# One row per routed token that carries weights and token number, two expert rows to a partition, loads ahead of the experts, and a sums buffer for each pair of batches

## The reference

```
probs = jax.nn.softmax(logits.astype(jnp.float32), axis=-1)
w_topk, sel = jax.lax.top_k(probs, K)
...
buf = jnp.zeros((E, CAP + 1, Hq), x.dtype).at[sorted_e, dest].set(x[tok])
g = jnp.einsum('ech,ehf->ecf', buf, w_gate)
u = jnp.einsum('ech,ehf->ecf', buf, w_up)
y = jnp.einsum('ecf,efh->ech', jax.nn.silu(g) * u, w_down)
wv = w_topk.reshape(-1)[order] * valid.astype(x.dtype)
out = jnp.zeros((T, Hq), x.dtype).at[tok].add(gath * wv[:, None])
sh = jax.nn.silu(x @ sw_gate) * (x @ sw_up) @ sw_down
sh = jax.nn.sigmoid(x @ w_shared_gate) * sh
```

## Time and profile before

| | us |
|---|---|
| median of 3 runs | 845.46 (843.39 to 845.92) |
| the profiled execution | 841.77 |
| its span in the profile | 839.5 |
| TensorE busy in it | 759.9 (91%) |
| VectorE, ScalarE, GpSimd busy | 544.3, 455.9, 493.8 |
| mean granted TensorE clock | 0.982 of full speed |

### The profile page before, as it was taken

How to read it: one execution, slowest core, us unless ns; L and a number is a source line. 1 busy time by engine, 2 the same in 40 slices (tenths; PEclk the granted TensorE clock), 3 DMA queues, 4 the chain that set the end, 5 groups by cost and what they waited for, 6 DMA issues and landing times.

```text
span 839.5 us, 12442 instructions
## 1 busy us (share of the span) xinstructions
PE 759.9 (91%) x3882; PEld 617.7 (74%) x3882; DVE 544.3 (65%) x1673; ACT 455.9 (54%) x1148; POOL 493.8 (59%) x400
## 2 busy tenths in 40 slices
PE   4688999999999999899999999999899858889957
PEld 2467888887888888788888788887676545667635
DVE  3398776688787978878787878895741223342433
ACT  4567876767876666697567777764521111111000
POOL 0445445453465588679578778857767555653560
PEclk9989999999999999999999999999999989999979
DMA  8906600000005010001301020403851299996270
GB/s 313 350 2 187 237 1 1 1 1 2 1 0 176 16 41 28 20 2 36 117 27 44 23 56 15 151 8 104 201 167 51 46 288 261 261 229 139 74 245 31
DMA packets 75152, 82.96 MB, mean 99 GB/s; under 512 B 8104, under 2 KB 65845, under 8 KB 75088
## 3 DMA queue, kind: packets, MB, share of 16 engines
q1 hardware_dynamic: 64208, 73.03, 28.3%
q0 software_dynamic: 9728, 8.46, 5.3%
q10 hardware_dynamic: 1152, 0.69, 0.3%
HBM read 54.37 MB, written 31.98 MB: 103 GB/s over the span
## 4 chain that ended last, share of the span: by engine, by line
PE 61%; DVE 14%; ACT 7%; issue 6%; DMA 6%; SPq 3%; POOL 2%; POOLq 0%; DVEq 0%; ACTq 0%
PE PJ L1271 17%; PE OUT L1369 9%; PE U L1358 5%; PE U L1324 5%; PE U L1515 4%; PE U L1347 4%; PE U L1359 2%; PE U L1323 2%; PE U L1271 2%; ACT U L521 2%; DMA xin<-in_dram 2%; DVE prob L927 2%; PE OUT L1460 2%; DMA xe<-slot_rows 2%; DVE U L917 2%
## 5 line engine op out<-in xcount | busy, mean ns | idle before, releaser
L709 POOL TENSOR_TENSOR qsw<-qsw,sinT 128x512 f32<-128x512 f32 x96 | 125.3, 1306 | 175.4 <-ACT qsw L508 174.2
L521 ACT ACTIVATE U<-U,nmax 128x128 f32<-128x128 f32 (+1 forms) x256 | 99.0, 387 | 94.5 <-DVE nmax L917 94.4
L1369 PE MATMUL OUT<-wo,oT 128*128 128x256 f32 x512 | 131.5, 380 | 0.0
L917 DVE CUSTOM_DVE_ANT_0 U<-U,mask 128x128 f32<-128x128 f32 (+1 forms) x256 | 86.6, 378 | 59.7 <-PE U L1324 59.3
L1271 PE MATMUL PJ<-hT_hi,w_hi 128*128 128x512 f32 x256 | 112.0, 437 | 0.8 <-issue 0.8
L1271 PE MATMUL PJ<-hT_lo,w_hi 128*128 128x512 f32 x256 | 101.3, 396 | 0.0
L1271 PE MATMUL PJ<-hT_hi,w_lo 128*128 128x512 f32 x256 | 101.0, 394 | 0.0
L713 POOL TENSOR_TENSOR qr<-qr,qsw 128x512 f32<-128x512 f32 x64 | 82.3, 1285 | 28.1 <-DVE qr L905 24.8
L927 DVE TENSOR_SCALAR prob<-U,rinv 128x128 f32<-128x128 f32 (+1 forms) x256 | 95.1, 413 | 4.5
L1369 PEld LDWEIGHTS OUT<-wo,oT 128*128 128x128 f32 x512 | 87.6, 191 | 6.6
L1358 PE MATMUL U<-pT,vN 128*128 128x256 f32 x256 | 78.3, 388 | 11.8 <-ACT pT L529 11.2
(11 more groups left out here) (199 smaller groups left out, 1651.8 us busy)
## 6 DMA issues: line engine op xcount, KB each, us to landing
wgu<-in_dram SPq DMA_DIRECT2D x32, 352.0 KB
expert_sum<-eq SPq DMA_DIRECT2D x3, 2176.0 KB, 17.8
sums<-expert_sum SPq DMA_DIRECT2D x12, 512.0 KB, 6.7
wd<-in_dram SPq DMA_DIRECT2D x16, 352.0 KB
wraw<-in_dram SPq DMA_DIRECT2D x8, 512.0 KB, 13.4
slot_rows<-eq SPq DMA_DIRECT2D x1, 4096.0 KB, 16.3
bcm<-mod_rows SPq DMA_DIRECT2D x8, 512.0 KB, 7.0
xe<-slot_rows SPq DMA_DIRECT2D x16, 256.0 KB, 8.3
```

Of the source, the lines that this page charges most:

```text
L521: last = act.activation(U[n % 3][:, a:z], U[n % 3][:, a:z], ACT.Exp, scale=-1.0, bias=nmax[:, n % 4, j:j + 1], accum_out=rsum[:, n % 4, j: ...
L709: pool.tensor_tensor(pair3(qsw[:, n % NQSW, :]), pair3(qsw[:, n % NQSW, :]), both(sinT[:, :]), ALU.mult).then_inc(t2_done, 1)
L917: last = dve.tensor_tensor_reduce(out=U[n % 3][:, a:z], in0=U[n % 3][:, a:z], in1=mask[:, a:z], scale=-float(HD) ** -0.5, scalar=3.4e38, o ...
L1369: last = pe.matmul(OUT[b][:, t * H:(t + 1) * H], oT[:, n % NOT, t * PN:(t + 1) * PN], wo[:, head, :], start=(head == 0 and t == 0), stop=( ...
```

## The change

The row that GpSimd scatters grows from 256 to 289 columns (ROW): the token's features, its 32 probabilities, its number as a float. The second scatter with all it needs (meta, eq, empty, post_pick, post_weights) goes. VectorE takes weight and number of two experts from the rows that were loaded (slot_w, slot_token, a semaphore told). An expert's weight rows 2p and 2p+1 now lie in partition p, which makes both next to each other in DRAM too; the transposes read every second column to match. SP's refill is split: rows, gate/up weights and down weights each wait for their own last use. gball and all four residual loads stand ahead of the wait for the scatters. sums and fin have a buffer for each pair; late_sums lies where the weight rings were. Beside it the zero fill writes rows of 1156 bytes.

```diff
+ROW = H + E + 1
+TOKEN = H + E
...
-            sp.dma_start(slots_d.rearrange("(a p) h -> p a h", p=PN),
-                         eq[:, 0:2, :, :].rearrange("p t k e -> p (t k e)").unsqueeze(1).broadcast_to([PN, E, H])).then_inc(st_zero, 16)
+            sp.wait_ge(fills, 9)
+            sp.dma_start(slots_d.rearrange("(s e) h -> s e h", e=E), blank[:, :].unsqueeze(1).broadcast_to([PN, E, ROW])).then_inc(st_zero, 16)
...
-            def expert_weights(e, i):
-
+            def gate_up_weights(e, i):
                 two = slice(2 * i, 2 * i + 2)
-                for dst, src in ((wgu[:, two, :, 0:F], w_gate), (wgu[:, two, :, F:2 * F], w_up)):
-                    sp.dma_start(dst.rearrange("p e c f -> p (e c) f"),
-                                 src[bass.ds(e, 2), :, :].rearrange("a (c p) f -> p (a c) f", p=PN)).then_inc(ld_e[i], 16)
-                sp.dma_start(wd[:, two, :, :].rearrange("p e c h -> p (e c) h"),
-                             w_down[bass.ds(e, 2), :, :].rearrange("a (c p) h -> p (a c) h", p=FH)).then_inc(ld_e[i], 16)
+                for g, src in enumerate((w_gate, w_up)):
+                    sp.dma_start(wgu[:, two, g, :, :].rearrange("p e c f -> p e (c f)"),
+                                 src[bass.ds(e, 2), :, :].rearrange("a (p c) f -> p a (c f)", p=PN)).then_inc(ld_gu[i], 16)
+
+            def down_weights(e, i):
+                two = slice(2 * i, 2 * i + 2)
+                sp.dma_start(wd[:, two, :, :].rearrange("p e c h -> p e (c h)"),
+                             w_down[bass.ds(e, 2), :, :].rearrange("a (p c) h -> p a (c h)", p=FH)).then_inc(ld_wd[i], 16)
...
             sp.wait_ge(st_base, 16 * NPAIR)
+            sp.wait_ge(st_xnt, 32 * NPAIR)
+            sp.wait_ge(lg_ps, NPAIR)
+            sp.dma_start(gball[:, :, :], mod_d[:, 3 * H:4 * H].partition_broadcast(PN)).then_inc(ld_gb, 16)
+            for q in range(NPAIR):
+                residual(q)
             sp.wait_ge(st_scat, 16 * NPAIR * TT * TOPK)
             for i in range(HALF):
                 slot_rows(2 * i, i)
-            sp.wait_ge(st_meta, 16 * NPAIR * TT * TOPK)
-            sp.dma_start(smeta[:, :, :].rearrange("p e c -> p (e c)"), meta_d.rearrange("(s e) c -> s (e c)", e=E)).then_inc(ld_meta, 16)
-            sp.dma_start(gball[:, :, :], mod_d[:, 3 * H:4 * H].partition_broadcast(PN)).then_inc(ld_gb, 16)
-            residual(0)
-            residual(1)
...
             for e in range(RING, E, 2):
+                i = (e // 2) % HALF
+                sp.wait_ge(xe_ps, e + 2 - RING)
+                sp.wait_ge(told, (e - RING) // 2 + 1)
+                slot_rows(e, i)
+                sp.wait_ge(gu_ps, e + 2 - RING)
+                gate_up_weights(e, i)
                 sp.wait_ge(ye_ps, e + 2 - RING)
-                slot_rows(e, (e // 2) % HALF)
-                expert_weights(e, (e // 2) % HALF)
+                down_weights(e, i)
...
-            expert_sums(0)
-            expert_sums(1)
             for q in range(NPAIR):
+                for i in range(NSUM):
+                    sp.dma_start(sums(q, i), acc_d[i][q * TOK:(q + 1) * TOK, :].rearrange("(t p) h -> p t h", p=PN)).then_inc(ld_sums[q], 16)
...
-            for c in range(TT * TOPK):
-                scatter_meta(LAST, c)
...
-                own(dve.tensor_tensor(ex[:, :, :], ex[:, :, :], red[:, 3, :].unsqueeze(2).broadcast_to([PN, TT, E]), ALU.mult))
+                dve.tensor_tensor(xn[:, :, H:H + E], ex[:, :, :], red[:, 3, :].unsqueeze(2).broadcast_to([PN, TT, E]), ALU.mult).then_inc(probs_done, 1)
...
+                    if n % 2 == 0:
+
+                        i = n % RING
+                        flat = xe[:, :, :].rearrange("p i r -> p (i r)")
+                        at = i * ROW + H + n
+                        dve.wait_ge(ld_xe[i // 2], 16 * (n // RING + 1))
+                        dve.tensor_copy(slot_w[:, n:n + 2], flat[:, at:at + ROW + 2:ROW + 1])
+                        dve.tensor_copy(slot_token[:, n:n + 2], xe[:, i:i + 2, TOKEN]).then_inc(told, 1)
...
-                        last = pe.transpose(PJ[n % 2][:, c * PN:(c + 1) * PN], xe[:, n % RING, c * PN:(c + 1) * PN], ident[:, :])
+                        last = pe.transpose(PJ[n % 2][:, c * PN:(c + 1) * PN], xe[:, n % RING, c:H:HC], ident[:, :])
```

More of the change, by code:

```diff
@@ L184, in adaln_block, with sums @@
         ye = sb("ye", [PN, RING, H])
-        smeta = sb("smeta", [PN, E, 2])
+        slot_w = sb("slot_w", [PN, E])
+        slot_token = sb("slot_token", [PN, E], I32)
         gball = sb("gball", [PN, B, H])
-        sums = sb("sums", [PN, 2, NSUM, TT, H])
-        fin = sb("fin", [PN, 2, TT, H])
+        fin = sb("fin", [PN, NPAIR, TT, H])
+        first_sums = sb("first_sums", [PN, NSUM, TT, H])
+        def sums(q, i):
+            return first_sums[:, i, :, :] if q == 0 else late_sums[:, q - 1, i, :, :]
         def bank(name):
@@ L443, in _ @@
                     sp.wait_ge(fin_done[q], 1)
-                    sp.dma_start(out[q * TOK:(q + 1) * TOK, :].rearrange("(t p) h -> p t h", p=PN), fin[:, q % 2, :, :]).then_inc(st_out[q % 2], 16)
+                    sp.dma_start(out[q * TOK:(q + 1) * TOK, :].rearrange("(t p) h -> p t h", p=PN), fin[:, q, :, :]).then_inc(st_out[q % 2], 16)
                 else:
@@ L447, in _ @@
                         sp.wait_ge(fin_done[q], t + 1)
-                        sp.dma_start(rows(out, q * TOK + t * PN), fin[:, q % 2, t, :]).then_inc(st_out[q % 2], 16)
[L449 to L452, removed]
+                        sp.dma_start(rows(out, q * TOK + t * PN), fin[:, q, t, :]).then_inc(st_out[q % 2], 16)
             sp.wait_ge(st_out[0], 16 * 2)
@@ L784, in _ @@
                 if l >= UNITS:
-                    for store, c in SCATTERS[l]:
-                        store(LAST - 1, c)
+                    for c in SCATTERS[l]:
+                        scatter(LAST - 1, c)
             post_base(LAST, 0)
@@ L828, in combine @@
             def combine(q):
-                a = sums[:, q % 2, 0, :, :]
-                pool.wait_ge(ld_sums[q % 2], 16 * NSUM * (q // 2 + 1))
+                a = sums(q, 0)
+                pool.wait_ge(ld_sums[q], 16 * NSUM)
                 for i in range(1, NSUM):
-                    own(pool.tensor_tensor(a, a, sums[:, q % 2, i, :, :], ALU.add))
+                    own(pool.tensor_tensor(a, a, sums(q, i), ALU.add))
                 own(pool.tensor_tensor(batches(a), batches(a), gate_of(q), ALU.mult))
-                f = fin[:, q % 2, :, :]
+                f = fin[:, q, :, :]
                 if q == 1:
@@ L1211, in expert_slot @@
                     dve.wait_ge(ye_ps, e + 1)
-                    if e == 0:
-                        dve.wait_ge(ld_meta, 16)
+                    dve.wait_ge(told, e // 2 + 1)
                     if e >= RING:
                         dve.wait_ge(st_acc[(e - RING) % NSUM], 16 * ((e - RING) // NSUM + 1))
-                    dve.tensor_scalar(ye[:, e % RING, :], YE[e % 2][:, 0:H], smeta[:, e, 0:1], None, ALU.mult).then_inc(ye_done, 1)
+                    dve.tensor_scalar(ye[:, e % RING, :], YE[e % 2][:, 0:H], slot_w[:, e:e + 1], None, ALU.mult).then_inc(ye_done, 1)
             def combine(q, step):
-                a = sums[:, q % 2, 0, :, :]
+                a = sums(q, 0)
                 if step < NSUM - 1:
                     if step == 0:
-                        dve.wait_ge(ld_sums[q % 2], 16 * NSUM * (q // 2 + 1))
-                    own(dve.tensor_tensor(a, a, sums[:, q % 2, step + 1, :, :], ALU.add))
+                        dve.wait_ge(ld_sums[q], 16 * NSUM)
+                    own(dve.tensor_tensor(a, a, sums(q, step + 1), ALU.add))
                 elif step == NSUM - 1:
@@ L1514, in expert_slot @@
                     for c in range(HC):
-                        last = pe.matmul(SC[e % 2][:, 0:2 * F], xeT[:, e % 2, c * PN:(c + 1) * PN], wgu[:, i, c, :],
+                        last = pe.matmul(SC[e % 2][:, 0:2 * F].rearrange("p (g f) -> p g f", g=2), xeT[:, e % 2, c * PN:(c + 1) * PN], wgu[:, i, :, c, :],
                                          start=(c == 0), stop=(c == HC - 1))
```

143 lines of the change are left out of this document (61 added, 82 removed).

## The result

The changed kernel takes 819.7 us (median of 4 runs, 817.21 to 826.83) against 845.69 us (4 runs, 843.39 to 846.36): a ratio of 0.9726, 95% interval 0.9684 to 0.9767. The execution profiled after took 817.21 us, the fastest of its four, with a span of 815.0 us against 839.5.

A forecast was written before the change was run, and what follows sets the result against it. TensorE was the engine to follow, with holes at the start, in the DMA-limited experts and in the tail. 20.7 + 11.9 + 0.8 - 2.0 = 31.4 us off 845.5 gave 814 us, own range 808 to 819, full 804 to 828.

The forecast's parts named there:

- the wider rows in the zero fill: Start, ahead of the second xin: the larger fill costs 2.0 us, bounds 1.4 and 10.9.
- if the fill takes far over 2 us more: Start: one of the signs named in advance that would show the forecast wrong.
- DMA lateness: Expert loop: at 6.1 us a pair of experts, TensorE ends 6.0 us late, bounds 0 and 17.
- Experts: Expert stage: 26.7 us gained with no stall, less 6.0 us of lateness, net 20.7 us.
- Tail: Behind the experts: a sums and fin buffer per pair removes the 12.9 us pause, net gain 11.9 us.
- The collision with GpSimd's additions: Tail: VectorE's adds may run beside GpSimd's and hold hs back, 1 us given back.
- Rival (c): Expert stage and tail: slower by slow-landing accumulates, deciding at L = 12.6 us; 850 us at 13; chance 0.03.
- zz and GpSimd: Behind the last pair: GpSimd's h products no longer run beside VectorE's zz, gain 0.8 us, bounds 0 and 1.
- Meta scatters in the pairs: Pairs of batches: the scatters cost TensorE nothing there, so removing them gains nothing.
- Strided transposes and the two small copies: Expert slots: 0 us taken; upper bounds 0.57 us a slot for strided loads, 0.35 us a pair for copies.
- rival (a): Expert stage: DMA keeps up fully, lateness 0, fill 1.4, no collision: gain 39, 806 us; chance 0.12.
- rival (b): Transfers stay dear: first case, a pair of 6.3 and fill of +5, 819 to 820; all upper bounds 834; chance 0.22.

The follow-up runs named there:

- Experiments 3: The changed kernel with rows of 320 floats (1280 bytes), pad columns zero: 817.22 us, ratio 0.9695.
- 4: The changed kernel with rows of 304 floats (1216 bytes), pad columns zero: 816.1 us, ratio 0.9687.
- 8: The changed kernel with rows of 1280 bytes, the fill writing only the first 1156 bytes of each: 816.29 us in one run.
- experiment 1: The changed kernel with the blank fill of slot_rows issued behind the load of the second pair's xin: 803.9 us, ratio 0.9529.
- Experiment 7: The changed kernel with the third and fourth pairs' sums and residual loads only behind the output of the first and second: 834.43 us, ratio 0.9899.
- experiments 2: The kernel before the change with its zero fill issued behind the load of the second pair's xin: 836.47 us, ratio 0.991.
- 12: The kernel before the change with only the split, earlier refill of slot rows and gate/up weights added: 843.22 us, ratio 0.9997.
- 11: The changed kernel with gball and four fin loads issued behind the first eight experts' slot rows again: 831.0 us, ratio 0.9862.
- experiment 10: The changed kernel with the fill behind the second xin, VectorE's last addition behind the first shrow, GpSimd's h products one step later: 804.91 us, ratio 0.9544.
- experiment 5: The changed kernel with the old expert weight layout, one row to a partition, early refills kept: 827.78 us, ratio 0.9801.

## Why the prediction was right, and where not

The forecast was 814 us, its own range 808 to 819, the full one 804 to 828; measured 819.7, inside the full range and just outside the narrow one. The sum was 31.4 us. Between the profiled executions it came to 24.5 (between the medians to 26.0). Point by point:

- *The term that was mis-sized is the wider rows in the zero fill: 2.0 us taken, 10.9 measured.* The bound of 10.9 ("twice the fill") was in the text; that it was hit to the decimal is chance, as the fill took 9.2 us longer (25.5 for 16.3) and not twice as long, with 1.7 us of other lateness behind it (0.6 of it low clock). The choice inside the bounds was wrong, and the text's own sign of it came: "if the fill takes far over 2 us more". It went by the nearest row in size, 704-byte packets that start on multiples of 64 bytes, while what mattered was where the rows lie. Experiments 3, 4 and 8 show that, and experiment 1 shows that the place of the fill made it cost anything at all.
- *DMA lateness: 6.0 us taken, 1.7 in the profiled execution.* The price of a joined packet was too dear: 6.1 us a pair stood for 3% of worth, where the run with the old layout shows a rate of 252 GB/s for 272 to 291. But single executions of this loop scatter by some 6 us, so 1.7 is its low end, and the median of after, 2.5 us over the profiled one, may hold more of it. Full engines to the end, TensorE late only for the last experts: as said, though it was late from slot 30 on and not from about 22.
- *Experts: 26.7 - 6.0 = 20.7 taken, 25.4 measured.* The first xe refill at 667.9 is 655.4 without the shift of 12.5 us, as forecast (655 to 657). The loads ahead, which the text gave no price of their own, cost as much to lose as the other two parts: 7.3 us of the expert stretch in the profile, 11 in the medians with what the clock adds.
- *Tail: 11.9 taken, 11.6 measured.* Experiment 7 shows the mechanism. The collision with GpSimd's additions was put at 1 us; the pauses for hs ahead of the down stages grew by 1.3. Rival (c), the accumulates, decided nothing: 7.5 us to land, as before; GpSimd waits 11.7 us for them and issues the last one 10 us behind the experts, so the loads of the sums start 13.6 us behind the experts and not 6, which the tail hides. The prediction's sum for (c) is off, too: by 703 + 10.7 L the kernel is as slow as before at 12.8 us, and at 13 it is 3 us slower, not 5.
- *zz and GpSimd: 0.8 taken.* zz takes 0.23 us for 1.15, as said. But in experiments 2 and 12, where GpSimd is as before, it takes 0.60 and 0.56, and the stretch to the first expert, 1.1 us shorter in this pair of profiles, takes 107.4 to 107.5 us in executions of both kinds (experiments 2 and 12 against 3, 7 and 11), all at a granted clock of 0.95. A gain of 0.3 to 0.9 us fits zz; the time doesn't show it.
- *Meta scatters in the pairs: nothing taken, 2.8 us lost.* The cover was named (the third pair of before, with its sixteen scatters, is not longer), but not what a scatter keeps apart (for 0.9 of the 2.8, by experiment 10).
- *Strided transposes and the two small copies: 0 taken, 0 measured.* Slots take 2.49 to 2.50 us. But the loads that read every second column are not free. They take 196 ns for 142, and in experiment 5, which reads the columns in turn again, 141; the 0 holds because they lie under matmuls, as the text said. First after, then experiment 5:

```profile
L1492 PEld LDWEIGHTS PJ<-ident,xe x64: 193/196/218, 666.7 to 742.1; 128*128 128x128 f32 x64
```
```profile
L1492 PEld LDWEIGHTS PJ<-ident,xe x64: 138/141/144, 667.8 to 750.6; 128*128 128x128 f32 x64
```

  The rule of full rate up to a stride of 4 fp32, which the prediction takes from the Trainium skill, "SBUF — State Buffer", section on the DMA port swizzle, is not borne out by these weight loads.

The miss of the fill (8.9) and of the pairs (2.8) was met in part by the experts (+4.7), most of it the lateness that only rival (a) had left out. That two errors of opposite sign met is luck: without it the time would lie some 10 us above the forecast. The direction was right, and the time lies 5.7 us above the forecast, at the edge of rival (b)'s first case, through (b)'s fill and not its transfers in the loop.

## What to carry to other kernels

Where a change widens rows in DRAM, look at the address of each row, not only at its bytes: padding 1156 to 1216 bytes made the same fill faster by 6 us. A bulk write that nobody waits for belongs behind the load that somebody does; that move alone was worth 16 us here. Where DMA is the limit of a stage, the worth of a part that saves or moves DMA time can depend on the others: undone one at a time three of them cost 6 to 11 us each, and the one that was tried alone gave nothing. And where the same loop takes 66 to 73 us from one execution to the next, one trace doesn't show what a part is worth.

## What the runs showed of the hardware

- Writes to DRAM of 1156 bytes at multiples of 1156 bytes take 25.5 us for 4624 KB; the same packets at multiples of 1280 bytes take 18.2 us. Rows of 1216 bytes, at multiples of 64, take 19.4 us for 4864 KB.
- TensorE's weight loads with a stride of two fp32 take longer than those without: 196 ns for 141 on 128 columns, 158 for 122 on 88.
- Taking work away from GpSimd made VectorE slower. Before, a meta scatter stood ahead of GpSimd's product on h; without it the product runs beside VectorE's two xn products, which then take 2.05 us for 1.04. With the products moved TensorE got 1.0 us back between the second prefix matmul and the third; between the first and the second it did not.
  The Trainium skill, "SBUF — State Buffer", section "Who interferes with whom", has it that a VectorE operation with two inputs in SBUF and a GpSimd one that reads SBUF block each other. The rows agree in that both slow down: GpSimd's product takes 1.45 us for 1.29.
- The granted clock fell in stretches in which TensorE worked without a gap, too. In the first experiment it was 0.50 and 0.59 in 610 to 620 us, with TensorE busy in all of it. It had paused for 1.97 and 0.57 us, until 597.4 and 603.6 us, and from 606.6 us on ran 2.3 us of matmuls of 34 columns, near whose end they take 0.38 us for 0.26. Such stretches ahead of the experts make 104.3 to 109.3 us of nearly the same work and blur every comparison here by some 3 to 5 us; what sets them off stays open.

```profile
605.00:610.00 5.00, 5.00 (x32) 4.29 (x31) 0.17 (x1) 1.76 (x2) 0.96 (x1) 0.88 0.94 308
610.00:615.00 5.00, 5.00 (x12) 3.30 (x11) 3.60 (x24) 0.37 (x2) 0.00 (x0) 0.50 0.99 323
615.00:620.00 5.00, 5.00 (x16) 3.76 (x15) 1.70 (x9) 0.47 (x1) 0.71 (x1) 0.59 0.87 173
```
